# Row factors of a layer norm: spread over the partitions by DMA through DRAM instead of by TensorE

## The reference, cut to what matters

```
q = silu(causal_dwconv(h @ Wq, qconv_w, qconv_b))
k = silu(causal_dwconv(h @ Wk, kconv_w, kconv_b))
q = (q - mean(q)) * rsqrt(var(q) + 1e-5) * qn_w + qn_b     # over the 128 features of a head, the same for k
S = (1 - b) * S + b * v k^T;  o = S q                      # per token
x = x + (o * silu(h @ Wg)) @ Wo
x = x + ffn(dense(x))
```

## Time and profile before

| | |
|---|---|
| median of 3 runs | 2692.74 us (2691.93 to 2693.76) |
| profiled execution | 2688.58 us, span 2687.0 us |
| busy share | PE 95%, VectorE 63%, ScalarE 45%, GpSimd 26% |
| DMA | 416 MB, 155 GB/s over the span, mean busy share of the queue's 16 engines 47.4% |

### The profile page before, as it was taken

One profiled execution on the slowest core, in us unless ns is written; L12 is line 12 of the kernel. 1 busy time (PEld: TensorE's weight loads), 2 busy tenths in 40 slices (PEclk: granted clock), 3 DMA queues, 4 the chain that ended last, 5 costly groups with the idle time before them and its releaser, 6 DMA issues.

```text
span 2687.0 us, 39946 instructions
## 1 busy us (share of the span) xinstructions
PE 2556.7 (95%) x14514; PEld 1986.7 (74%) x14536; DVE 1688.0 (63%) x2848; ACT 1197.1 (45%) x1878; POOL 693.9 (26%) x764
## 2 busy tenths in 40 slices
PE   5889999999999999999999999999999999999996
PEld 4667777777777777777777777777777777777764
DVE  3766666666666666666656666666666666666653
ACT  3555544544444444454444444353444544344431
POOL 3455522212222212222212222222222212222220
PEclk8999999999999999999999999999999999999998
DMA  5775744445344544355354454444444455344430
GB/s 161 255 223 187 239 154 157 139 160 176 121 140 151 161 162 157 111 170 190 117 174 128 147 176 154 148 139 152 159 145 148 140 163 175 125 139 152 155 129 16
DMA packets 264554, 416.17 MB, mean 155 GB/s; under 512 B 102058, under 2 KB 126634, under 8 KB 264362
## 3 DMA queue, kind: packets, MB, share of 16 engines
q1 hardware_dynamic: 264362, 413.63, 47.4%
HBM read 360.86 MB, written 52.69 MB: 154 GB/s over the span
## 4 chain that ended last, share of the span: by engine, by line
PE 88%; DVE 4%; ACT 3%; issue 2%; SPq 1%; POOL 1%; DMA 1%; ACTq 0%; DVEq 0%; POOLq 0%
PE ring L1050 31%; PE pj_a L1050 25%; PE pj_b L1050 13%; PE ring L1266 4%; PE m L1256 3%; PE var L1224 2%; PE cen_q L1245 2%; PE cen_k L1245 1%; PE cen_k L1246 1%; PE cen_q L1246 1%; PE ring L1151 1%; PE ring L1068 1%; ACT hb L914 1%; PE var L1235 1%; PE m L1266 1%
## 5 line engine op out<-in xcount | busy, mean ns | idle before, releaser
L782 DVE SCALAR_TENSOR_TENSOR y_q<-pj_a,conv,y_q 128x504 f32<-128x504 f32 (+2 forms) x384 | 281.7, 733 | 361.6 <-ACT y_q L965 352.5
L500 POOL TENSOR_TENSOR og_lo<-gt,og_hi 128x512 fp32r<-128x512 f32 x128 | 165.0, 1289 | 929.5 <-ACT og_hi L995 929.5
L1050 PE MATMUL pj_a<-ht_hi,wg 128*128 128x512 f32 x1024 | 352.9, 405 | 3.2 <-DVE y_q L782 3.2
L1050 PE MATMUL pj_a<-ht_hi,wq 128*128 128x512 f32 x1024 | 346.2, 400 | 2.3 <-DVE ht_lo L628 1.5
L1050 PE MATMUL pj_b<-ht_hi,wk 128*128 128x512 f32 x1024 | 336.2, 389 | 0.0
L1050 PE MATMUL ring<-wo,og_hi 128*128 128x512 f32 x1024 | 321.4, 395 | 14.8 <-DVE acc L662 11.8
L1050 PE MATMUL ring<-wv,ht_hi 128*128 128x512 f32 x1024 | 320.7, 394 | 6.8 <-ACT hb L916 6.8
L782 DVE SCALAR_TENSOR_TENSOR y_k<-pj_b,conv,y_k 128x504 f32<-128x504 f32 (+2 forms) x384 | 281.8, 734 | 62.2 <-ACT y_k L965 53.1
L953 ACT ACTIVATE sq_q<-cen_q 128x512 f32<-128x512 f32 x128 | 76.5, 598 | 449.6 <-PE cen_q L1246 449.5
L1050 PEld LDWEIGHTS ring<-wo,og_hi 128*128 128x128 f32 x1024 | 190.4, 189 | 74.2 <-DVE acc L662 18.5
L1050 PEld LDWEIGHTS ring<-wv,ht_hi 128*128 128x128 f32 x1024 | 189.2, 188 | 73.9 <-issue 26.8
(11 more groups left out here) (202 smaller groups left out, 5078.6 us busy)
## 6 DMA issues: line engine op xcount, KB each, us to landing
wq<-parts_q SPq DMA_DIRECT2D x112, 512.0 KB, 3.9
wk<-parts_k SPq DMA_DIRECT2D x112, 512.0 KB, 4.3
wg<-parts_g SPq DMA_DIRECT2D x112, 512.0 KB, 3.6
wv<-parts_v SPq DMA_DIRECT2D x112, 512.0 KB, 6.4
wo<-parts_o SPq DMA_DIRECT2D x112, 512.0 KB, 6.1
keep<-keep_rows SPq DMA_DIRECT2D x256, 64.0 KB, 3.6
wo<-parts_w SPq DMA_DIRECT2D x28, 512.0 KB, 5.8
acc<-in_x_dram SPq DMA_DIRECT2D x8, 1024.0 KB, 5.5
```

What stands on the lines that cost most here:

```text
L500: G.tensor_tensor(og_lo[:, u % OG_RING, :], gt[:, u % GT_RING, :], og_hi[:, u % OG_RING, :].bitcast(F32), ALU.subtract).then_inc(S["oglo"], 1)
L782: V.scalar_tensor_tensor(out=yy[:, :, k:], in0=pp[:, :, :L - k], scalar=conv[:, i, h, 3 - k:4 - k], in1=yy[:, :, k:], op0=ALU.mult, op1=AL ...
L1050: last = T.matmul(psum, a, b, start=start and n == 0 and m == 0, stop=stop and n == len(pairs) - 1 and m == 2)
```

## The change

`rstd` is no longer split and no longer spread by matmuls. SP writes its four rows to a small DRAM tensor `r_rows`, waits for the write, and reads each row back to all 128 partitions, 256 KB a row, into the buffer `sq` whose squares the variance has read. `normalise` reads these. The variance matmuls go in front of the projection of k, ACT's seed in front of the first tap of k, and DVE's Newton step in front of the taps of k. `squares` now waits until `normalise` has used the factors of two units before. 7 instructions of DVE's set-up go.

```diff
+            def load_rstd(m):
+                sp.wait_ge(S["rr"], m + 1)
+                for j in range(4 if m else 0):
+                    sp.wait_ge(S[f"r_in_{'qk'[j % 2]}{j // 2}"], 16 * m)
+                sp.dma_start(r_rows, rstd[0:P:32, :]).then_inc(S["r_out"], 16)
+                sp.wait_ge(S["r_out"], 16 * (m + 1))
+                for j in range(4):
+                    x_ = "qk"[j % 2]
+                    sp.dma_start(sq[x_][:, j // 2, :], r_rows[j:j + 1, :].broadcast_to([P, GROUP])).then_inc(S[f"r_in_{x_}{j // 2}"], 16)
...
                 if h == 8 and 1 <= g < GROUPS:
                     for part in range(SET):
                         load_o(g * SETS, part)
+                if U % 2 == 0 and 2 <= U <= UNITS:
+                    load_rstd(U // 2 - 1)
                 if H <= U + 1 < UNITS:
                     load_head("g", U + 1)
...
@@ VectorE @@
-            def split_rstd(m):
             def normalise(u):
                 for x_ in "qk":
-                    dve.wait_ge(S[f"bc_{x_}"], u + 1)
+                    dve.wait_ge(S[f"r_in_{x_}{u % 2}"], 16 * (u // 2 + 1))
...
-                    V.tensor_tensor(c, c, bc_banks[u % 2][x_][:], ALU.mult)
+                    V.tensor_tensor(c, c, sq[x_][:, u % 2, :], ALU.mult)
...
                     taps("q", U)
+                if U % 2 == 0 and 2 <= U <= UNITS:
+                    newton(U // 2 - 1)
+                if U < UNITS:
                     taps("k", U)
...
@@ ScalarE @@
             def squares(x_, u):
                 if u > 1:
-                    act.wait_ge(S["var"], u // 2)
+                    act.wait_ge(S[f"n_{x_}"], u - 1)
...
             def seed(m):
-                    act.wait_ge(S["r_split"], m)
+                    act.wait_ge(S["r_out"], 16 * m)
-            def rstd_hi(m):
...
+                if U % 2 == 0 and 2 <= U <= UNITS:
+                    seed(U // 2 - 1)
                 if U < UNITS:
                     first_tap("k", U)
...
@@ TensorE @@
                 project("q", U)
-                    project("k", U)
                 if U % 2 == 0 and 2 <= U <= UNITS:
                     variance(U // 2 - 1)
-                if U % 2 and 0 <= U - 2 < UNITS:
-                    spread(U - 2)
+                if U < UNITS:
+                    project("k", U)
...
-                if U % 2 == 0 and 2 <= U <= UNITS:
-                    spread(U - 2)
```

More of the change, by code:

```diff
@@ L113, in adaln_attn_ffn @@
     parts_w2 = nc.dram_tensor("parts_w2", [KC, P, 2, 512], F32).ap()
+    r_rows = nc.dram_tensor("r_rows", [4, GROUP], F32).ap()
     gamma_row = nc.dram_tensor("gamma_row", [D], F32).ap()
@@ L137, in adaln_attn_ffn @@
         rstd = sb("rstd", [P, GROUP])
-        r_parts = sb("r_parts", [P, GROUP], F32R)
         keep = sb("keep", [P, 2, HALF])
@@ L162, in adaln_attn_ffn @@
         mean = sb("mean", [P, 32])
-        pick = sb("pick", [P, 4, P], F32R)
         conv = sb("conv", [P, 2, H, 5])
@@ L171, in adaln_attn_ffn @@
         eps_ln = sb("eps_ln", [P, 1])
-        is_low = sb("is_low", [P, 1])
-        signs = sb("signs", [P, 4, 1])
         st = sb("st", [P, 12, HT])
@@ L181, in adaln_attn_ffn @@
         pj = {"q": pj_a, "k": pj_b, "g": pj_a}
-        bc_banks = [{"q": var, "k": pj_b}, cen]
         w2_src, ffn_src = acc[:, 1], v[:, 1]
@@ L187, in adaln_attn_ffn @@
         sums_out = tern[:, 0:2, :].rearrange("p k d -> p (k d)").bitcast(F32)
-        ones = sq["q"][:, 0, 0:P]
         TAB_LOADS, LATE_LOADS = 4 + 4 + 1, 1 + KC + 2
-        SETUP_DVE, LATE_GAMMA, LATE_TERN = 22, 8, 22
+        SETUP_DVE, LATE_GAMMA, LATE_TERN = 15, 8, 22
         names = """tab_in late_in dense_in subj_in wb_in gamma_out w2_out setup_pool setup_dve setup_act late_dve
@@ L195, in adaln_attn_ffn @@
             w_hi_done w_split ring_mm0 ring_mm1 ring_free0 ring_free1
-            proj_q proj_k proj_g cen_q cen_k var scores bc_q bc_k weighed
+            proj_q proj_k proj_g cen_q cen_k var scores r_out r_in_q0 r_in_k0 r_in_q1 r_in_k1 weighed
             tap0_q tap0_k tap_q tap_k silu_q silu_k shi_q shi_k slo_q slo_k gated
-            sq_q sq_k cc_q cc_k seed newton_a newton_b rr r_hi r_split n_q n_k aff_q aff_k
+            sq_q sq_k cc_q cc_k seed newton_a newton_b rr n_q n_k aff_q aff_k
             scanned og_odd oghi oglo ht_hi beta_done keep_done x2_hi xam_mul xam_hi xam_lo ssq absmax small
@@ L554, in _ @@
             dve.wait_ge(S["setup_pool"], 8)
-            by32 = ident[:].rearrange("p (a b) -> p a b", b=32)
             step(V.tensor_scalar(mean[:], ident[:, 0:32], 0.0, 1.0 / P, ALU.mult, ALU.add))
@@ L562, in _ @@
                     step(V.tensor_copy(ident_in[half, t, :], ident[half, half]))
[L563 to L567, removed]
             dve.wait_ge(S["wb_in"], 16)
@@ L799, in newton @@
                                        ).then_inc(S["rr"], 1)
-            def split_rstd(m):
-                dve.wait_ge(S["r_hi"], m + 1)
-                V.scalar_tensor_tensor(out=r_parts[:], in0=rstd[:], scalar=is_low[:], in1=r_parts[:].bitcast(F32),
-                                       op0=ALU.mult, op1=ALU.subtract).then_inc(S["r_split"], 1)
             def normalise(u):
                 for x_ in "qk":
-                    dve.wait_ge(S[f"bc_{x_}"], u + 1)
+                    dve.wait_ge(S[f"r_in_{x_}{u % 2}"], 16 * (u // 2 + 1))
                     dve.wait_ge(S[f"cc_{x_}"], u + 1)
                     c = c_[x_][:, u % C_RING, :]
-                    V.tensor_tensor(c, c, bc_banks[u % 2][x_][:], ALU.mult).then_inc(S[f"n_{x_}"], 1)
+                    V.tensor_tensor(c, c, sq[x_][:, u % 2, :], ALU.mult).then_inc(S[f"n_{x_}"], 1)
             def weigh(u):
@@ L839, in _ @@
                 take(U, 0)
-                if U % 2 == 0 and 2 <= U <= UNITS:
-                    newton(U // 2 - 1)
                 if 0 <= U - 3 < UNITS:
@@ L845, in _ @@
                     silu_lo("k", U)
-                if U % 2 == 0 and 2 <= U <= UNITS:
-                    split_rstd(U // 2 - 1)
                 take(U, 1)
@@ L1020, in _ @@
                     silu("q", U)
-                if U % 2 == 0 and 2 <= U <= UNITS:
-                    seed(U // 2 - 1)
                 take(U, 0)
@@ L1028, in _ @@
                     silu("k", U)
-                if U % 2 == 0 and 2 <= U <= UNITS:
-                    rstd_hi(U // 2 - 1)
                 for b in blocks:
@@ L1209, in project @@
                     pe.wait_ge(S["tap_k"], 3 * u)
-                    if u % 2 and u > 2:
-                        pe.wait_ge(S["n_k"], u - 2)
                 elif x_ == "g":
@@ L1221, in variance @@
                 if m:
-                    pe.wait_ge(S["n_q"], 2 * m - 1)
+                    pe.wait_ge(S["rr"], m)
                 for j in range(4):
@@ L1225, in variance @@
                 mm.then_inc(S["var"], 1)
[L1227 to L1236, removed]
             def centre(x_, u):
@@ L1242, in centre @@
                     pe.wait_ge(S[f"sq_{x_}"], u)
-                if u % 2 and u > 2:
-                    pe.wait_ge(S[f"n_{x_}"], u - 1)
                 T.matmul(cen[x_][:], center[:], s_hi[x_][:], start=True, stop=False)
```

## The result

The changed kernel takes 2730.63 us (median of 4 runs, 2729.39 to 2731.44) against 2692.34 (4 runs, 2690.01 to 2693.76), 38 us more. The ratio on record is 1.0151 [1.0138, 1.0164]; it fits the lowest of the four, 2690.01, and so do the runs of the kernel before in the experiments (medians 2689.2 to 2689.6). 2683 was predicted. The profiled execution has a span of 2727.7 us against 2687.0, and a mean granted clock of 0.967 of full speed against 0.985.

What follows compares the result with a forecast made beforehand. TensorE, busy for 95% of the span, was taken as the bound. The terms -58 - 6 + 43 + 11 = -10 us took the profiled 2688.6 to 2678.6; with 4.2 for the median, about 2683, range 2636 to 2716.

Steps and rivals of the forecast that it cites:

- Spread removed: On TensorE, four groups of 64 spread matmuls go, about 0.46 us in each slot: -58 us.
- split-factor wait: TensorE's idle time ahead of spread goes, booked for group 0 and the tail: -6 us, bounds 0 and -27.
- Variance moved: Variance ahead of the projection of k: the projection of q covers its wait for the squares of k, cost nothing.
- Seed and Newton moved: Taps of k and silu of q start later, level again by `s_lo` of k: nothing, bounds -0.3 to +0.5 us a slot.
- Round trip in ordinary slots: In ordinary even slots the row of k lands just in time for normalise: cost 0, upper bound 100 us.
- Rival 2: The trip misses the slack in ordinary even slots too: +32 us, about 2715, chance 0.28.
- h8 and h9: Factors queue behind h8's wo loads; TensorE idles 8 to 9 us in h9, then loses clock: +43 us, bounds 0 and +60.
- Rival 3: h8 costs only the lag and no clock: -27 us, about 2666; no chance of its own, within the forecast's range.
- Rival 1: The write isn't held by the wo loads in h8, factors in time everywhere: -53 us, about 2637, chance 0.2.
- Group 0: The trip comes 4 us late for normalise, some 1.3 past VectorE's slack, in six slots: +3 us.
- h12: Outputs, x, its matrices and then wq go out behind 1 MB more of reads: +4 us.
- slot 18: Two loads of 512 KB stand in front of the trip; booked the same as group 0, +3 us.

Runs made afterwards that it cites:

- no_trip: The changed kernel without the DRAM write and reads; normalise multiplies by the squares left in `sq`, so the factors are not applied: 2664.83 us.
- g0_neither: The changed kernel with the trip before h8's wo loads, variance, seed and Newton at old places up to slot 18, no trip in group 0: 2663.72 us.
- moves_only: The kernel before with variance, seed and Newton moved forward, split and spread kept: 2708.28 us.
- h8_first: The changed kernel with the write and reads issued ahead of the four wo loads in h8: 2693.42 us.
- cond_early: The changed kernel, trip before h8's wo loads, moved steps at old places up to slot 18, next group's small matrices loaded in h11: 2673.45 us.

## Why the prediction failed, step by step

- **Spread removed, -58; split-factor wait, -6.** Too large. The matmuls went, and most slots are 0.5 us shorter. But in h0, h6 and h10 the length did not change, with the trip or without it (`no_trip`), because the saving comes back as a wait at attend (0.5 to 1.1 us instead of 0 to 0.6). Three slots in each of seven groups at 0.46 are 10 us. And group 0 without trip and moves (`g0_neither`) is 5.7 us shorter, where the two terms have 13. "Work taken from TensorE pays in full wherever it runs without a gap" left out that at attend another engine was only just in time.
- **Variance moved, 0.** Right: in U=66 all is as worked out, and the later groups of `moves_only` are not longer.
- **Seed and Newton moved, 0.** This is one of the two steps that failed most. The argument was made on U=66, where GpSimd is idle most of the time. In group 0, GpSimd splits the weights between the halves of q and k, and each delay of silu of q goes on to `s_lo` of k and to centring. Measured 11 to 17 us by the profiles and 8 by the medians; with `spread` kept, 35 by the profile and 19 for the whole kernel.
- **Round trip in ordinary slots, 0.** Right. VectorE waited for the row of q 15 times in 64 trips: six times in group 0 (3.0 to 4.1 us), in slot 18 (8.8), in the seven h8 (3.0 to 4.2) and in the tail (4.2). Elsewhere it waited once for the row of k (0.9 us, slot 62), and ordinary slots did not grow. Rival 2 is wrong: the result was on its side of zero, but for another reason. The 2.0 us that the prediction took from the Trainium skill, page "DMA: Bandwidth & Descriptors", section "Anatomy of one DMA", are that section's fit for transfers issued by GpSimd. Here SP issues them, and from the write's issue to the first read it took 1.7 us at least.
- **h8 and h9, +43.** Right in mechanism and size: h8 and h9 together +5.1 us a group against +5.2 worked out, the idle stretch up to 8.2 us, and 2.5 us lost at half clock behind it, where 2.4 had been taken. `h8_first` gives back 37 us. Rival 3, the lag without the clock, does not fit the windows at 0.50 and 0.83. Rival 1 is excluded: the 8 KB did not overtake the 2 MB. Its price was wrong as well: without any trip h8 and h9 together are still 0.6 us a group longer than before, since TensorE, now early, waits 4 us for VectorE in h9 (`no_trip`). The Trainium skill, page "DMA: Bandwidth & Descriptors", section "Queues, rings and completion order", has each DMA engine take its descriptors in ring order; the 6.3 us agree with it.
- **Group 0, +3.** The other step that failed most, 15 to 21 us measured. The row of slot 10 was right, a wait of some 4 us in six slots. But not only VectorE's slack counts: squares of the next slot now wait for normalise too, and on SP the raw weights stand behind the trip. In slot 12 of the changed kernel (timeline):
```profile
289.46 0.55 SPq L338 DMA_DIRECT2D r_rows<-rstd  x1
...
295.17 0.69 DVE L807 TENSOR_TENSOR c_q<-c_q,sq_q 128x512 f32<-128x512 f32 x1 [3.78 <-DMA sq_q<-r_rows]
295.81 9.17 SPq L315 DMA_DIRECT2D cond_pair<-in_L_cond_weights_dram  x8
295.95 0.60 ACT L948 ACTIVATE sq_q<-cen_q 128x512 f32<-128x512 f32 x1 [6.06 <-DVE c_q L807]
```
  ScalarE stands 6.06 us, and then once 8.0 us more for a raw half of Wq, whose load SP issues behind the trip, x and the matrices. That the 8 us come from this order, and how the 21 us divide over the chains, no run separates.
- **h12, +4, and slot 18, +3.** The first is too small: h14 grew by 0.8 to 2.1 us in six groups where 0.46 should have been saved, about 11 us. It is `wq` that comes late there; `no_trip`, where h14 is 0.5 us shorter, shows that the trip is needed for it, and `cond_early` that the loads of the small matrices are. The second came out near its size by luck: slot 19 grew by 3.8 us, on a wait of 3.3 us for `wq` (slot 18 got 1.5 us shorter), but it grew by the same 3.8 us in `no_trip`, so the trip is not its cause. Why `wq` is late there, no run shows.

Against the forecast 51 us are missing: 36 in group 0 (moves, trip, and a smaller saving), 10 that attend takes back and 7 in h14; small differences elsewhere make up the rest. So the step that failed is the price of group 0: the moves were put at 0 from U=66, and the trip at +3 from VectorE's slack alone. The runs show some 30 us there in place of these 3. The price of the trip in h8, and in the ordinary slots, came out as worked out.

## What to carry to other kernels

Work out a moved instruction in the stretch where each engine behind it is fullest, not in the typical slot: in the warm-up group GpSimd's weight splits stood in the path, and one eighth of the kernel made most of the loss. A DRAM round trip on one queue costs what stands ahead of it (6.3 us behind 2 MB, 1.7 us ahead of them), so place it ahead of large loads, and bring forward what it needs where it would come late (here only h14). When a wait is removed and the gain comes back later in the same engine's time, look for a chain that the wait had covered; here moving that chain gained 22 us with the wait removed and cost 8.6 us with it in place.

## What the runs showed of the hardware, not expected

- **GpSimd slows when VectorE reads two operands from SBUF.** The same affine on POOL, of q and k, before and after (count | busy, mean ns):
```profile
L507 POOL TENSOR_SCALAR c_q<-c_q,ln_q 128x512 f32<-128x512 f32 x128 | 116.8, 912 | 372.2 <-DVE c_q L811 372.2
L507 POOL TENSOR_SCALAR c_k<-c_k,ln_k 128x512 f32<-128x512 f32 x128 | 101.1, 790 | 0.0
```
```profile
L514 POOL TENSOR_SCALAR c_q<-c_q,ln_q 128x512 f32<-128x512 f32 x128 | 140.3, 1096 | 419.8 <-DVE c_q L807 419.8
L514 POOL TENSOR_SCALAR c_k<-c_k,ln_k 128x512 f32<-128x512 f32 x128 | 125.3, 979 | 4.4 <-DVE c_k L807 4.4
```
  Normalise now reads SBUF and SBUF instead of SBUF and PSUM. `no_trip`, with no DMA into `sq`, has 1113 and 992 ns, and `moves_only`, with PSUM, 915 and 783. So it is the operand, not the transfer. One by one, the affine of q took 0.77 us beside a normalise of k that reads PSUM (59 times), 0.77 us with VectorE idle, and 1.14 to 1.29 us beside one that reads SBUF twice (57 times). The affine of k is pushed back by this and now starts while VectorE's scan, which also reads SBUF twice, is running: 1.13 to 1.23 us instead of 0.77. Why the engines hold each other up was not tried by itself.
- **VectorE slows beside GpSimd's splits as well:** in slot 12 `s_lo_k` took 0.69 us with GpSimd idle (kernel before) and 1.74 when it started 0.07 us after GpSimd's split of `wk` (`moves_only`). Where VectorE had started first, at 271.62, it was GpSimd's split of `wk` that took 1.83 us instead of 1.26.
- **A small write has no fixed latency.** From the issue of 8 KB to the next read's issue SP needed 1.7 to 2.0 us in h8 ahead of the wo loads, 5.5 to 6.4 behind their 2 MB, and 1.7 to 4.2 in the other slots of groups 1 to 7.
